# Flamingo block with a routed FFN: shared slots interleaved with the last routed slots, tiles finished in natural order

## The reference, cut to what matters

```python
x = x + tanh(g_xattn) * mamba_like_scan(ctx_1024, layernorm(x), ...)
h = layernorm(x)                                  # 2048 tokens, H = 512
combine = top2(softmax(h @ gate_w.T))             # E = 16 experts, K = 2
y = sum_e combine[:, e] * (swiglu(h @ w_gate_up[e]) @ w_down[e])   # I = 352
y = y + swiglu(h @ shared_gate_up) @ shared_down                   # SI = 704
return x + tanh(g_ffn) * y
```

## Time and profile before

| | |
|---|---|
| median of 3 runs | 1107.25 us (1105.29 to 1111.7) |
| the profiled execution's own time | 1106.53 us |
| its span | 1104.9 us |
| busy, share of the span | PE 83%, DVE 66%, ACT 55%, POOL 54% |
| mean granted TensorE clock | 0.918 |
| chain that ended last, PE's share of the span | 40% |

### The profile page before, as it was taken

How to read it: one execution, slowest core, us unless ns; L and a number is a source line. 1 busy time by engine, 2 the same in 40 slices (tenths; PEclk the granted TensorE clock), 3 DMA queues, 4 the chain that set the end, 5 groups by cost and what they waited for, 6 DMA issues and landing times.

```text
span 1104.9 us, 22746 instructions
## 1 busy us (share of the span) xinstructions
PE 920.2 (83%) x5388; PEld 776.6 (70%) x5389; DVE 728.1 (66%) x1023; ACT 611.2 (55%) x1037; POOL 594.0 (54%) x521
## 2 busy tenths in 40 slices
PE   6589876998689877974799989699999999973787
PEld 3267655765567566753799979698988898862775
DVE  4769798878888788998544467354544545444467
ACT  4697997599778977993322222243444544432211
POOL 4557796878967796996100007334344424420254
PEclk9579998999999978998899999899999999995789
DMA  8105111331105113110311118645556656653376
GB/s 254 40 20 191 59 36 33 138 109 30 39 28 199 49 29 109 56 48 20 117 38 38 51 36 296 242 137 204 184 197 216 216 203 233 206 176 111 116 220 236
DMA packets 67432, 137.08 MB, mean 124 GB/s; under 512 B 9392, under 2 KB 15024, under 8 KB 67248
## 3 DMA queue, kind: packets, MB, share of 16 engines
q1 hardware_dynamic: 54736, 105.66, 28.5%
q0 software_dynamic: 8960, 29.37, 7.4%
q10 hardware_dynamic: 3680, 1.39, 0.6%
HBM read 163.53 MB, written 42.07 MB: 186 GB/s over the span
## 4 chain that ended last, share of the span: by engine, by line
PE 40%; issue 4%; DVE 4%; POOL 3%; DMA 1%; ACT 1%; DVEq 0%; POOLq 0%
PE psY L956 12%; PE psG L920 11%; PE psU L920 10%; PE psT L913 3%; POOL slot_in L625 3%; PE psHT L934 3%; DVE x_tok L1864 1%; ACT xh L1290 1%; DMA gbuf<-slot_out,posi 0%; PE dbu_ps L767 0%; DVE hl L1676 0%; DVEq L1841 0%; DVE xl L1682 0%; PE y_ps L785 0%; POOL gbuf L672 0%
## 5 line engine op out<-in xcount | busy, mean ns | idle before, releaser
L573 POOL TENSOR_TENSOR prod<-hst,cbc 128x512 f32<-128x512 f32 x256 | 333.0, 1327 | 84.8 <-PE y_ps L785 66.9
L1476 DVE TENSOR_TENSOR_SCAN hst<-dA,dbu_ps 128x512 f32<-128x512 f32 x256 | 304.0, 1208 | 67.8 <-PE dbu_ps L767 57.8
L767 PE MATMUL dbu_ps<-ident,dbuT 128*128 128x128 f32 x1024 | 169.9, 292 | 38.5 <-ACT dbuT L1173 16.8
L767 PEld LDWEIGHTS dbu_ps<-ident,dbuT 128*128 128x128 f32 x1024 | 124.9, 149 | 104.6 <-issue 49.7
L1296 ACT CAST hh<-psHT 128x384 fp32r<-128x384 f32 x79 | 37.8, 478 | 288.8 <-PE psHT L934 288.8
L1162 ACT ACTIVATE dA<-dts,Aneg 128x512 f32 (+1 forms) x256 | 169.3, 712 | 33.2 <-DVE hst L1476 32.7
L1173 ACT ACTIVATE dbuT<-duT,BT 128x512 f32 (+1 forms) x256 | 163.0, 709 | 0.0
L785 PE MATMUL y_ps<-ident,prod 128*128 128x128 f32 x1024 | 160.7, 284 | 2.1 <-POOL prod L573 2.0
L920 PE MATMUL psG<-weights,xh 128*128 (+1 forms) x560 | 142.3, 337 | 14.8 <-issue 8.5
L956 PE MATMUL psY<-weights,hh 128*128 (+3 forms) x420 | 135.7, 405 | 16.7 <-DVE hl L1676 14.3
L920 PE MATMUL psU<-weights,xh 128*128 (+2 forms) x560 | 143.1, 337 | 0.0
(11 more groups left out here) (220 smaller groups left out, 1389.4 us busy)
## 6 DMA issues: line engine op xcount, KB each, us to landing
raw_gu<-in_L_ffn_w_gate_up_dram SPq DMA_DIRECT2D x100, 704.0 KB
raw_d<-in_L_ffn_w_down_dram SPq DMA_DIRECT2D x50, 512.0 KB
cbc<-c_rows SPq DMA_DIRECT2D x64, 256.0 KB, 3.2
slot_in<-ztile SPq DMA_DIRECT2D x3, 4096.0 KB, 13.7
gbuf<-slot_in SPq DMA_DIRECT2D x48, 256.0 KB, 3.1
slot_out<-yout POOLq DMA_DIRECT2D x48, 256.0 KB, 3.2
raw_d<-in_L_ffn_w_down_dram SPq DMA_DIRECT2D x50, 192.0 KB
xn_rows<-xin SPq DMA_DIRECT2D x16, 256.0 KB, 2.0
```

The lines of the kernel that those rows point to most:

```text
L573: pool.tensor_tensor(prod[:, prod_slot(n, j), :], hst[:, slot_of(n, j), :], cbc[:, n % 2, :], ALU.mult).then_inc(prod_ready, 1)
L767: last = tr(dbu_ps[j % 2][:, t * P:(t + 1) * P], dbuT[:, n % 2, t, j * P:(j + 1) * P], ident[:])
L1476: V.tensor_tensor_scan(hst[:, slot_of(n, j), :], dA[:, slot_of(n, j), :], dbu_ps[j % 2][:], 0.0, ALU.mult, ALU.add).then_inc(scanned, 1)
```

## The change

The last eight routed slots (r = 40 to 47, from `R1 = SLOTS - 8`) are written out in four pairs, and behind pair g comes the shared slot of tile 8 + g (`NMIX = 4`, `mixed_q`). Four shared slots, tiles 12 to 15, are left for the end (from `QA`). TensorE's loops now end at slot 39, those of ScalarE, VectorE, GpSimd and SyncE too. Gathers, finishing and output stores go in natural tile order 0 to 15. VectorE finishes none after the first of the last four slots, tiles 0, 1 after the second, 2, 3 after the third, 4, 5, 6 after the fourth, and 7 to 15 behind the last `hl`. No transfer, matmul or elementwise instruction is added or dropped: the same 80 slots, 32 gathers and 32 finishing instructions are reordered.

```diff
+        R1, NMIX = SLOTS - 8, 4
+        QA = NT + NB1 + SLOTS + NMIX
+        def routed_q(r):
+            return NT + NB1 + r + (max(r - R1, 0) // 2 if isinstance(r, int) else 0)
+        def mixed_q(g):
+            return NT + NB1 + R1 + 3 * g + 2
 # SyncE
-            with sp.Fori(0, SLOTS // 4 - 1) as m:
+            with sp.Fori(0, R1 // 4) as m:
...
+            for g in range(2):
+                load_tile(tile_rows(xn_rows, NB1 + g), Q0, g)
+            for r in range(R1, SLOTS):
+                g = (r - R1) // 2
+                if r + 4 < SLOTS:
+                    sp.wait_ge(xT_done, routed_q(r) + 1)
+                    load_slot(r + 4, r % 4)
                 prefetch_expert(r)
+                if r % 2 == 1:
+                    load_tile(tile_rows(xn_rows, NB1 + g + 2), mixed_q(g) + 2, g % 2)
+            for n in range(NB1 + NMIX + 2, NT):
+                load_tile(tile_rows(xn_rows, n), QA + n - NB1 - NMIX, n % 2)
 # GpSimd
-                t = (i % 2) * NB1 + i // 2
+            for t in range(NT):
+                if t >= 4:
+                    pool.wait_ge(f_done, t - 3)
 # TensorE
-            with pe.Fori(FULL // 4, SLOTS // 4 - 1) as m:
+            with pe.Fori(FULL // 4, R1 // 4) as m:
...
+            for g in range(NMIX):
+                r = R1 + 2 * g
...
+                before, before_used = routed_slots(r, 2, pair_source, before=before, before_used=before_used,
+                                                   full=False, q0=routed_q(r), first=upcoming)
...
+                slot(mixed_q(g), g % 2, 2, before % 2,
+                     routed_rows(r + 2, (r + 2) % 4) if more else loaded(NB1 + NMIX, 0),
+                     prev_rank=before, before_down=read_ahead if more else None, prev_used=before_used)
+            for n in range(NB1 + NMIX, NT):
+                slot(QA + n - NB1 - NMIX, n % 2, 2, 2, loaded(n + 1, (n + 1) % 2) if n < NT - 1 else None)
 # VectorE
+            for g in range(NMIX):
+                r = R1 + 2 * g
...
+                    routed_slot(r, g % 2, routed_q(r), "shared", NB1 + g - 1)
+                routed_slot(r + 1, (g + 1) % 2, routed_q(r + 1))
+                slot(mixed_q(g), g % 2, "routed", r + 1)
...
+            finished = iter(range(NT))
+            for n, also in ((0, 0), (1, 2), (2, 2), (3, 3)):
+                t = NB1 + NMIX + n
+                slot(QA + n, n % 2, "shared", t - 1, last_slot=n == 3)
+                for _ in range(also):
+                    finish(next(finished))
+            h_lo(QE - 1, 1)
+            for t in finished:
+                if t == NT - 1:
+                    result_to(QE - 1, 1, "shared", NT - 1)
+                if t >= NB1 + NMIX:
+                    tile_read(t)
+                finish(t)
```

More of the change, by code:

```diff
@@ L654, in rest_lo @@
                     ins.then_inc(d_split, 1)
-            with pool.Fori(0, SLOTS // 2) as m:
+            with pool.Fori(0, R1 // 2) as m:
                 for k in range(2):
@@ L661, in _ @@
                                    yout[:, k, :]).then_inc(y_stored[k], 16)
+            for r in range(R1, SLOTS):
+                rest_lo(r)
+                pool.wait_ge(y_read, routed_q(r) + 1 + 2)
+                pool.dma_start(slot_out[bass.ds(r * P, P), :], yout[:, r % 2, :]).then_inc(y_stored[r % 2], 16)
             pool.wait_ge(y_stored[0], 16 * (SLOTS // 2))
@@ L1022, in read_used, with routed_slots @@
                 return pe.value_load(used_i[0:1, bass.ds(r, 1)], min_val=0, max_val=1)
-            def routed_slots(r0, n, source, before=None, before_used=None, full=True):
-                ranks = [before, read_rank(r0)]
-                used = [before_used, None if full else read_used(r0)]
+            def routed_slots(r0, n, source, before=None, before_used=None, full=True, q0=None, first=None):
+                if first is None:
+                    first = read_rank(r0), None if full else read_used(r0)
+                if q0 is None:
+                    q0 = r0 + Q0
+                ranks = [before, first[0]]
+                used = [before_used, first[1]]
+                k0 = q0 % 2 if isinstance(q0, int) else 0
                 def read_next():
@@ L1336, in down_hi, with routed_slot @@
                     split_d_hi(128 + 32 * r, dst)
-            def routed_slot(r, k, first=False):
-                slot(r + Q0, k)
-                if not first:
+            def routed_slot(r, k, q, late_down=True):
+                slot(q, k)
+                if late_down:
                     down_hi(r - 1)
@@ L1835, in _, with routed_slot @@
             slot(Q0 - 1, 1, "shared", NB1 - 2, late=True)
-            def routed_slot(r, k, kind="routed"):
+            def routed_slot(r, k, q, kind="routed", t=None):
                 table = {}
@@ L1842, in read_tables @@
                     table["rank"] = dve.value_load(rank_i[0:1, bass.ds(r, 1)], min_val=0, max_val=NE)
-                slot(r + Q0, k, kind, r - 1 if kind == "routed" else NB1 - 1, before_result=read_tables)
+                slot(q, k, kind, r - 1 if kind == "routed" else t, before_result=read_tables)
                 rank = table["rank"]
@@ L1866, in finish @@
                     if c == 0:
                         ins.then_inc(f_first, 1)
-                        dve.wait_ge(f_first, i + 1)
+                        dve.wait_ge(f_first, t + 1)
                 ins.then_inc(f_done, 1)
[L1871 to L1887, removed]
-            h_lo(QE - 1, 1)
-            finish_pair(NB1 - 2, QE - 2, 0)
```

108 lines of the change are left out of this document (47 added, 61 removed).

## The result

The changed kernel takes 1115.68 us (median of 8 executions, 1114.3 to 1118.07), the kernel before, measured beside it, 1106.97 (8 executions). The ratio is 1.0084, 95% interval 1.0064 to 1.0104: slower by 0.8%, 8.7 us on these medians. The profiled execution took 1115.99 us, its span is 1114.2, so the spans differ by 9.3.

A forecast was written before the change was run, and what follows sets the result against it. The end was taken as an empty-slot latency chain, a TensorE stall, then a tail of nearly equal gathers and shared slots. 10.6 - 8.8 + 2.0 = +3.8 us on 1107.25 gave 1111.0; 8-in-10 range 1103 to 1118.5.

The forecast's parts named there:

- the mark: End of the up product of the shared slot following r = 47; predicted to come 10.6 us later.
- the forecast case: Main case for the whole kernel, 1111.0 us, ranging from 1105 to 1115; chance 0.62.
- Part 1: Stretch up to the mark: predicted 10.6 us later, with three more shared slots done.
- The lost edge: Second edge of TensorE's four-slot loop, among the empty slots: predicted gone, 3.1 us.
- A group: One pair of empty slots plus a shared slot, mark to mark: predicted 11.9 us.
- Part 2: Stretch from the mark to the end: predicted 57.5 us instead of 66.3, 8.8 less.
- The pitch: Spacing of GpSimd's 32 tail gathers: predicted 0.95 us busy and 0.30 of issue each.
- Part 3: TensorE's clock in the interleaved groups: 2.0 us added, between bounds of nothing and 8.4.
- The clock falls in every group: Rival: gaps between interleaved groups lower TensorE's clock, sum +10.2 us, 1117.5; chance 0.23.
- Skips stall: Rival: straight-code empty slots stall when jumping over products, 3.1 us per pair, 12.4 in all, 1123.5; chance 0.06.
- The pairs hide: Rival: shared work covers both empty chains, a group takes 8.4 us, 1098.5; chance 0.09, including gathers not binding.
- The gathers don't bind: Rival: TensorE, not the gathers, sets the end, nearly the time of hidden pairs; chance within their 0.09.

The follow-up runs named there:

- The early load: Changed kernel with the loads of tiles 8 and 9 put ahead of SyncE's loop over routed slots; ratio to the kernel before 1.0067.
- the ring of six: Changed kernel with gather buffers for six tiles instead of four, so gathers wait for the finishing six tiles before; ratio to the kernel before 1.0123.
- half the gathers: Changed kernel without each tile's second gather, the first one's rows added twice; ratio to the kernel before 0.9996.
- before itself: The kernel before, unaltered, run again for its trace on an experiments' chip; ratio to the kernel before 1.0015.
- the order alone and 32 in a row: Kernel before with tiles in natural order, VectorE's end written out, and a buffer for each of 32 gathers; ratio to the kernel before 1.0244.

## Why the prediction was right, point by point

The sign and the mechanism held: the mark comes later by more than the tail gets shorter. The size, +3.8 against +9.3 between the profiled spans, was low by 5.5: 1.6 ahead of the change, 1.7 up to the mark and 4.2 behind it were missing, and 2.0 for the clock was not needed. The measured 1115.68 lies above the 1115 to which the forecast case reached. It lies within the range of 1103 to 1118.5 because that had been widened for the clock and for skips, and neither of them happened in this trace. That part of the agreement is luck.

**Ahead of the change.** Predicted: nothing. Measured: 1.6. It grows bit by bit, from 0.6 us at the first slots (ScalarE's copies at 656.26 and 656.86) to 2.2 at r = 38, over code that is the same in both, less the 0.7 of the edge. The single executions of the kernel before spread over 6.4 us (1105.29 to 1111.7). What makes the 1.6 stays open.

**Part 1, 10.6 predicted, 12.3 measured.** The lost edge is right; that the other edge costs what turning costs is not quite, it took 6.21. The wait for tile 8's load was mis-sized: I had the load issued behind r = 39's weights early enough to land 0.9 late. (1001.18 + 2.6 is 1003.8, not 1003.6; that slip is 0.2 of it.) SyncE's queue issued it at 1003.39, it landed 2.6 later, and the transposes were at 1006.06: counted from the edge 0.9 later than predicted. The early load confirms that it is a wait of this size. The first slot at the low clock took 7.2 (7.44 predicted). A group took 12.2 against 11.9, in three of them 0.9: the steps from one up product's end to the next were 0.68, 2.10, 2.14, 2.40 and 4.89 against 0.9, 1.7, 2.2, 2.5 and 4.6. The mis-sized ones are those two whose price I had from a slot at another place, the way from transposes to down product (2.10 for 1.7) and the gate and up products that start from a standing TensorE (4.89 for 4.6). 0.9 - 0.2 + 0.9 = 1.6, within 0.1 of the difference.

**Part 2, 57.5 predicted, 61.7 measured.** Everything about its structure held: no stall of VectorE ahead of an `hl`, first gather at 4.8 (5.2), waits for finished tiles at tiles 4, 6 and 8 (4.6 in sum, under the 6 that I had set; the prediction counts four waits but names these three), no further one of more than 0.3, gathers to the last. Two terms were mis-sized. The pitch: seven gathers without a wait took 1.14 to 1.47 us instead of the 0.95 in the earlier trace rows, 2.4 us more in sum, nearly all of the difference between 49.5 and 51.9. And the way from the last gather to the end: I added a landing of 3.8 from one row and an output store of 2.6 from another, with the finishing 7.9. Measured 3.80 + 1.54 + 4.50 = 9.8. Before had the same 9.8 in another split, 5.6 + 1.5 + 2.6, as two subtractions in the earlier trace rows would have told me (1095.13 to 1104.9). In eleven of the fourteen traces of the table this way is 9.25 to 9.9, whatever its split. What sets the sum was not tested.

**Part 3, 2.0 predicted, none in the profiled execution.** The groups ran at 1.00, so the rule in the Trainium skill (TensorE: Matmul & The Clock Gate, "A second HAM failure mode: psum-queue depth-cycling"), that small idles between groups can make the clock swing, gives too much for this trace. It isn't wrong for the kernel, however. The windows view of the changed kernel on the other chip, group by group (length, PE busy, granted clock, DMA share, GB/s):

```profile
1032.98:1047.86 14.88, 11.61 (x55) 0.81 0.39 112
1047.86:1061.71 13.85, 10.54 (x54) 0.88 0.18 59
1061.71:1075.57 13.86, 10.52 (x55) 0.88 0.18 62
```

and of the ring of six, whose slots are the same up to there:

```profile
1047.07:1059.36 12.29, 8.96 (x54) 1.00 0.22 72
1059.36:1073.22 13.86, 10.52 (x54) 0.88 0.18 60
```

A group either runs at 1.00 in 12.2 to 12.3 us or loses 1.6 at 0.88. Of the second and third groups of the six experiments with four pairs, six of twelve fell; of the first chip's profiled execution none of two. So the term is a matter of the execution, 0 to 3.2 us in these two groups, and its middle was near what I took. What decides which group falls is open. The changed kernel's way from r = 40 to the first gather is 2.4 us longer on the other chip (58.00 against 55.57): 3.2 for two fallen groups and 0.3 for the first group (14.88 against 14.60), less 1.0 for a shorter wait for tile 8's load (5.87 against 6.91 to its gate product).

**The rivals.** *The clock falls in every group*: half true, see above; it would have cost 3.2, not 8.4, in the groups behind the first. *Skips stall*: false, no "issue" of over 1 us stands in front of TensorE in the pairs; the rule in the Trainium skill (Runtime: NRT & Kernel Launch, "Instruction fetch mechanics"), that a taken branch out of the blocks at hand waits for its fetch, did not show here. It isn't refuted either, since no run tells where the blocks end. *The pairs hide*: false, 12.2 against the 9.5 at which it would decide. *The gathers don't bind*: false, shown by half the gathers, 11.7 us less from the first gather on.

## What to carry to other kernels

Work moved out of a tail pays only until the next resource in it binds: count what else must pass through the tail (here 32 gathers at 1.26 us plus 10 us behind the last), and move no more than brings the first engine down to that. What is put ahead of the moment that starts that resource costs in full; here each interleaved group delayed the first gather by 12.2 - 7.7 = 4.5 us. And take the way from the last transfer to the end as one difference out of one trace, not as a sum of parts whose samples come from different rows.

## What the runs showed that I had not expected

**Engines that stand while indirect DMAs are issued back to back.** In the traces of the first chip no wait is marked remote. In all twelve of the experiments, on the three chips, there are such waits (whether it is the chip that makes the difference isn't known) where GpSimd issues indirect DMAs without a pause, in the scatter too, for the kernel before as for all others. ScalarE's timeline there, first of the changed kernel on the first chip, then the same copy of the same kernel on another:

```profile
676.94 0.48 ACT L1326 CAST hh<-psHT 128x384 fp32r<-128x384 f32 x1 [5.30 <-PE psHT L949]
```

```profile
709.23 0.48 ACT L1326 CAST hh<-psHT 128x384 fp32r<-128x384 f32 x1 [33.72 <-remote]
```

The scatter's 32 issues end at 704.83 there; 4.4 us later ScalarE goes on. Two copies earlier the two traces are 1.1 us apart (664.64 and 663.55), at this one 32.3, and at the SiLU of r = 40 25.4 (1027.11 and 1001.74). So most of what these chips take longer comes from the scatter; in the kernel before that SiLU is at 1027.21 instead of 1000.15. ScalarE's waits grow with the length of the unbroken row of issues (8 gathers in the changed kernel, none in the tail; 12, 13.4 us in before itself and 14.4 in the ring of six; 32, 39.7 us), and in the changed kernel with all 32 in a row the wait ended 4.8 us behind the last. With the order alone and 32 in a row VectorE's last one ended 4.6 behind, while ScalarE, in its loop, went on at 1093.5, 15 us ahead of the last. VectorE has remote waits of 2.3 to 4.4 us behind rows of 8 too. What the engines wait for is open: some of the expectations above took it for code that comes late, and no run tested that apart. On these chips the four-tile ring with its waits for finished tiles, which I had taken for a cost of 5 us, so also holds the gathers back to a pace at which ScalarE goes on.

**The clock of one group.** The same 54 matmuls with the same gaps took 12.29 or 13.86 us in successive groups of one execution.
